# Query and key projections of a gated attention kernel: three rounded products over the whole array in place of float32 products in two column tiles

## The reference

```
xn = layernorm(x)
Q, K, V = xn @ Wq, xn @ Wk, xn @ Wv          # 16 heads of 64, per batch of 1024 tokens
A = softmax(Q K^T / 8) V                      # per batch and head
s = xn + gelu(A) @ Wpost
g = silu(quantise(xn) @ quantise(W).T + bias) # blocks of 32, values on a 6-bit grid
out = x + s * g
```

## Time and profile before

| | |
|---|---|
| median of 3 runs | 1372.78 us (1372.38 to 1373.0) |
| profiled execution, its own time | 1374.83 us |
| its span, first to last instruction | 1372.9 us |
| busy: PE, PEld, DVE, ACT, POOL | 1354.9, 740.5, 1099.5, 768.4, 1169.5 us |
| mean granted PE clock | 0.995 of full speed |
| DMA | 87.61 MB, 64 GB/s |

### The profile page before, as it was taken

The page is one execution under the profiler, slowest core; times in us unless marked ns, Lnnn a source line. Parts: engine busy times, 40 slices in busy tenths (PEclk is TensorE's granted clock), DMA queues, the critical chain, the costliest instruction groups (busy, mean ns, idle before and its releaser), DMA issues.

```text
span 1372.9 us, 26059 instructions
## 1 busy us (share of the span) xinstructions
PE 1354.9 (99%) x9828; PEld 740.5 (54%) x9828; DVE 1099.5 (80%) x1499; ACT 768.4 (56%) x1059; POOL 1169.5 (85%) x548
## 2 busy tenths in 40 slices
PE   7899999999999999999999999999999999999998
PEld 4455555555455555555555555555555555555588
DVE  6688888888888888888888888888888888888533
ACT  3455665554556666455555666555554655555583
POOL 1589999889999989989999999899999999999950
PEclk8999999999999999999999999999999999999999
DMA  2012122111212112121211112121111111222374
GB/s 83 17 42 64 45 62 72 49 57 57 64 42 65 57 45 77 57 64 42 65 56 51 56 57 64 42 64 56 48 58 57 49 27 49 64 77 60 90 258 144
DMA packets 110488, 87.61 MB, mean 64 GB/s; under 512 B 70430, under 2 KB 84510, under 8 KB 110364
## 3 DMA queue, kind: packets, MB, share of 16 engines
q1 hardware_dynamic: 110364, 85.96, 20.7%
HBM read 69.66 MB, written 16.25 MB: 63 GB/s over the span
## 4 chain that ended last, share of the span: by engine, by line
PE 96%; DVE 2%; DMA 1%; issue 0%; ACT 0%; SPq 0%; POOL 0%; DVEq 0%
PE acc L526 32%; PE scores L507 26%; PE peaks L486 13%; PE extra L408 9%; PE scores L516 6%; PE extra L421 4%; PE scores L596 4%; DVE half_maxes L957 1%; PE extra L450 1%; DMA sums<-sum_scratch 1%; PE extra L457 1%; PE extra L432 0%; DMA sum_scratch<-group_sums 0%; DMA x_in<-in_L_attn_X 0%; DVE group_sums L993 0%
## 5 line engine op out<-in xcount | busy, mean ns | idle before, releaser
L840 POOL TENSOR_TENSOR prob_sum<-prob_sum,probs 128x1024 f32<-128x1024 f32 x384 | 915.1, 2383 | 89.3 <-ACT probs L711 49.3
L957 DVE TENSOR_REDUCE half_maxes<-peaks 128x2 f32<-128x1024 f32 x504 | 616.2, 1223 | 182.0 <-PE peaks L486 176.3
L711 ACT ACTIVATE probs<-scores 128x1024 f32<-128x1024 f32 x357 | 355.7, 1024 | 474.5 <-PE scores L516 464.8
L526 PE MATMUL acc<-probs,vals 128*64 128x512 f32 x2048 | 486.1, 595 | 0.0
L526 PEld LDWEIGHTS acc<-probs,vals 128*64 128x64 f32 x2048 | 139.0, 137 | 234.8 <-issue 225.9
L486 PE MATMUL peaks<-k_hi,q_hi 64*128 64x512 f32 x1008 | 233.3, 457 | 4.5 <-DVE half_maxes L957 4.1
L486 PEld LDWEIGHTS peaks<-k_hi,q_hi 64*128 64x128 f32 x1008 | 95.5, 184 | 208.6 <-issue 142.6
L507 PE MATMUL scores<-q_hi,k_hi 64*128 64x512 f32 x1024 | 203.4, 393 | 0.0
L507 PE MATMUL scores<-q_hi,k_lo 64*128 64x512 f32 x1024 | 203.3, 392 | 0.0
L507 PE MATMUL scores<-q_lo,k_hi 64*128 64x512 f32 x1024 | 202.7, 391 | 0.0
L840 POOL TENSOR_TENSOR prob_sum<-probs 128x1024 f32<-128x1024 f32 x64 | 153.5, 2399 | 57.0 <-ACT probs L711 57.0
(11 more groups left out here) (156 smaller groups left out, 923.0 us busy)
## 6 DMA issues: line engine op xcount, KB each, us to landing
max_rep<-max_scratch SPq DMA_DIRECT2D x62, 512.0 KB, 4.0
inv_sum<-inv_scratch SPq DMA_DIRECT2D x128, 128.0 KB, 2.9
att_scratch<-att SPq DMA_DIRECT2D x48, 256.0 KB, 2.3
probs<-att_scratch SPq DMA_DIRECT2D x8, 512.0 KB, 5.0
max_scratch<-turned SPq DMA_DIRECT2D x252, 1.0 KB
sums<-sum_scratch SPq DMA_DIRECT2D x128, 8.0 KB, 2.1
xTs<-att_scratch SPq DMA_DIRECT2D x4, 512.0 KB, 3.6
out_dram<-xn SPq DMA_DIRECT2D x8, 256.0 KB, 3.3
```

Source lines behind the costliest of these rows:

```text
L526: last = mm(acc[own[h], :], vals[(s // 2) % 2][:, j, own[h]], probs[j][:, h, :], start=(k == 0), stop=(k == KT - 1), tile_position=col[h])
L711: sa.activation(probs[j][:, :, :], src[:, :, :], ACT.Exp, scale=DH ** -0.5).then_inc(probs_ready, 1)
L840: gp.tensor_tensor(prob_sum[s % 2][:, :, :], before[:, :, :], probs[order(s)[j]][:, :, :], ALU.add).then_inc(probs_summed, 1)
L957: v.tensor_reduce(half_maxes[:, :, f // 2, f % 2], peaks[:, :, :], AX.X, ALU.max).then_inc(peaks_read, 1)
```

## The change

Four things are changed together.

- **Projections.** For every pair but the first, the queries and keys are projected as three float32r products over the whole array (hi·hi, weights hi·x lo, weights lo·x hi) that accumulate in the bank, three instructions in all, in place of float32 products in two column tiles, four instructions. Values stay as they are.
- **Splits.** x and the two weights are split into a rounded part and a remainder. At the start ACT rounds all of x of batch 0 and both weights, and POOL subtracts three tiles of 128 x 1024. At each of the three turns to a new batch, ACT rounds two halves and DVE subtracts two halves.
- **Memory and order at the turn of a batch.** There is one transposed x in place of four, so the next batch's transposes move from pairs 4 and 5 to pair 6 of the batch (rounds 1 and 3 of its half-1 step), and the first query projection of the new batch moves behind `weigh`. `w_q` and `w_k` share memory with the last two attention blocks, the squares go to `xn`, and of the first eight loads of attention blocks, which stood one a step and then two and one, one stays at step 56, three go to step 61 and four to step 62.
- **First step.** The twelve peaks of step 0 are made three a round, not four, four, two, two. The joining of the maxima of step 1 moves from round 1 to round 2.

```diff
-            if r == 1 and n % HP in (4, 5) and n // HP + 1 < B:
-                before.append(("x", n // HP + 1, n % HP - 4))
+            turned_now = n % HP == HP - 2 and n // HP + 1 < B
+            if r in (1, 3) and turned_now:
+                before.append(("x", n // HP + 1, r // 2))
...
-                before.append(("q", n + 2, 0))
+                (behind if turned_now else before).append(("q", n + 2, 0))
...
     def fills(s, r):
-        if s == 0 and r < 2:
-            return [(1, 4 * r + i) for i in range(4)]
+        if s == 0:
+            return [(1 + k // 8, k % 8) for k in range(3 * r, 3 * r + 3)]
...
-                for p in {NS - 3: (5, 6), NS - 2: (7,)}.get(s, (s - NS + 8,)):
+                for p in {NS - 8: (0,), NS - 3: (1, 2, 3), NS - 2: (4, 5, 6, 7)}.get(s, ()):
...
+                if n == 0:
+                    weights = w_q if name == "q" else w_k
+                    pe.wait_ge(w0_loaded, 48)
+                    has_xT(0, half)
+                    for h in (0, 1):
+                        last = mm(w[own[h], :], weights[:, h * DH:(h + 1) * DH], xT[:, halves[half]],
+                                  start=True, stop=True, tile_position=col[h])
+                else:
+                    if n // HP == 0:
+                        pe.wait_ge(first_split, 3)
+                    else:
+                        pe.wait_ge(x_split, 2 * (n // HP) - 1 + half)
+                    w_hi, w_lo = (wq_hi, wq_lo) if name == "q" else (wk_hi, wk_lo)
+                    for i, (left, right) in enumerate(((w_hi, xT_hi), (w_hi, xT_lo), (w_lo, xT_hi))):
+                        last = mm(w[:, :], left[:, at:at + P], right[:, halves[half]], start=(i == 0), stop=(i == 2))
...
+            def round_xT(use):
+                _, b, half = use
+                is_read(act, use)
+                sa.copy(xT_hi[:, halves[half]], xT[:, halves[half]]).then_inc(x_rounded, 1)
...
+            act.wait_ge(xT_ready, 2)
+            sa.copy(xT_hi[:, :], xT[:, :]).then_inc(x_rounded, 2)
+            act.wait_ge(w0_loaded, 48)
+            act.wait_ge(w_loaded, 48)
+            for dst, weights in ((wq_hi, w_q), (wk_hi, w_k)):
+                sa.copy(dst[:, :], weights[:, :]).then_inc(w_rounded, 1)
...
-                    if half == 1 and r == 1 and n % HP in (4, 5) and later < B:
-                        copy_xT_later(("x", later, n % HP - 4))
+                    if half == 1 and r in (1, 3) and n % HP == HP - 2 and later < B:
+                        copy_xT_later(("x", later, r // 2))
+                    if half == 1 and r == 2 and n % HP == HP - 2 and later < B:
+                        round_xT(("x", later, 0))
+                    if half == 0 and r == 0 and n % HP == HP - 1 and later < B:
+                        round_xT(("x", later, 1))
...
+            pool.wait_ge(x_rounded, 2)
+            gp.tensor_tensor(xT_lo[:, :], xT[:, :], xT_hi[:, :], ALU.subtract).then_inc(first_split, 1)
+            for k, (hi, lo, weights) in enumerate(((wq_hi, wq_lo, w_q), (wk_hi, wk_lo, w_k))):
+                pool.wait_ge(w_rounded, k + 1)
+                gp.tensor_tensor(lo[:, :], weights[:, :], hi[:, :], ALU.subtract).then_inc(first_split, 1)
...
+            def low_x(use):
+                _, b, half = use
+                dve.wait_ge(x_rounded, 2 * b + half + 1)
+                v.tensor_tensor(xT_lo[:, halves[half]], xT[:, halves[half]], xT_hi[:, halves[half]], ALU.subtract).then_inc(x_split, 1)
...
+                    if half == 0 and r == 0 and n % HP == HP - 1 and later < B:
+                        low_x(("x", later, 1))
...
+                    if half == 1 and r == 2 and turned_now:
+                        low_x(("x", later, 0))
+                    if half == 1 and r == 3 and turned_now:
+                        low(("q", n + 2, 0))
```

More of the change, by code:

```diff
@@ L105, in gated_attention_kernel @@
         sem = lambda n: ctx.enter_context(nc.semaphore(n))
-        w_q, w_k, w_v = (sb(f"w_{n}", [P, HD]) for n in "qkv")
-        xT = [sb(f"xTs{b}", [P, S]) for b in range(B)]
+        w_v = sb("w_v", [P, HD])
+        xT = sb("xTs", [P, S])
         with ExitStack() as rounded:
@@ L116, in gated_attention_kernel @@
         rows_back = [sb(f"rows_back{z}", [P, HALF]) for z in (0, 1)]
+        split_back = [sb(f"split_back{k}", [P, S]) for k in range(6)]
         maxima, turned = sb("maxima", [P, SQ], F32R), sb("turned", [P, SQ])
@@ L157, in gated_attention_kernel @@
         flat = lambda a: a[:, :, :].rearrange("p a b -> p (a b)")
-        back = [flat(x_in), flat(squares), xT[0][:, :], xT[1][:, :], xT[2][:, :], xT[3][:, :], w_q[:, :], w_k[:, :],
+        back = [flat(x_in), xT[:, :]] + [split_back[k][:, :] for k in range(6)]
+        back += [
                 q_hi_back[0][:, :], q_lo_back[0][:, :], k_hi_back[0][:, :], k_lo_back[0][:, :],
@@ L420, in project_v @@
                         tokens = half * HALF + t * P + h * DH
-                        last = mm(w[own[h], t * P:(t + 1) * P], xT[n // HP][:, tokens:tokens + DH], w_v[:, at:at + P],
+                        last = mm(w[own[h], t * P:(t + 1) * P], xT[:, tokens:tokens + DH], w_v[:, at:at + P],
                                   start=True, stop=True, tile_position=col[h])
@@ L632, in square @@
                 act.wait_ge(centred, p + 1)
-                sa.activation(squares[:, t0:t0 + nt, :], x_in[:, t0:t0 + nt, :], ACT.Square).then_inc(squared, 1)
+                sa.activation(xn[b][:, t0:t0 + nt, :], x_in[:, t0:t0 + nt, :], ACT.Square).then_inc(squared, 1)
             def root(p):
@@ L671, in copy_xT @@
                 is_filled(act, use)
-                sa.copy(xT[b][:, halves[half]], bank(use)).then_inc(xT_ready, 1)
+                sa.copy(xT[:, halves[half]], bank(use)).then_inc(xT_ready, 1)
             def copy_xT_later(use):
@@ L676, in copy_xT_later @@
                 is_filled(act, use)
-                sa.copy(xT[b][:, halves[half]], bank(use)).then_inc(extra_read, 1)
+                sa.copy(xT[:, halves[half]], bank(use)).then_inc(extra_read, 1)
+            def round_xT(use):
+                _, b, half = use
+                is_read(act, use)
+                sa.copy(xT_hi[:, halves[half]], xT[:, halves[half]]).then_inc(x_rounded, 1)
             def high(use):
@@ L745, in _ @@
                         copy_v(("v", n + 1, 0))
-                    if n + 2 < NP and half == 1 and r == 3 and not gates_now:
+                    if n + 2 < NP and half == 1 and r == 3 and not gates_now and not (n % HP == HP - 2 and later < B):
                         high(("q", n + 2, 0))
@@ L759, in _ @@
                         copy_acc(s - 1)
+                    if half == 1 and r == 3 and n % HP == HP - 2 and later < B:
+                        high(("q", n + 2, 0))
                     if half == 1 and r == 1:
@@ L1050, in _ @@
                         low(("q", 1, 0))
-                    if r == 1 and s > 0 and s + 1 < NS:
+                    if r == (1 if s > 0 else 2) and s + 1 < NS:
                         join_maxima(s + 1)
@@ L1058, in _ @@
                         low((("k", n + 1, 0), ("k", n + 1, 1), ("q", n + 1, 1))[r])
-                    if n + 2 < NP and half == 1 and r == 3:
+                    turned_now = n % HP == HP - 2 and later < B
+                    if n + 2 < NP and half == 1 and r == 3 and not turned_now:
                         low(("q", n + 2, 0))
-                    if r == 1 and s > 0 and s + 1 < NS:
+                    if r == (1 if s > 0 else 2) and s + 1 < NS:
                         turn_squares(s + 1)
```

22 lines of the change are left out of this document (11 added, 11 removed).

## The result

The changed kernel takes 1380.3 us (median of 5 runs, 1379.4 to 1382.8), the kernel before 1373.0 beside it (5 runs): ratio 1.005, 95% interval 1.0038 to 1.0062. It is slower by 7.3 us, where 3.1 were forecast. The median lies 0.3 above the forecast's range of 1350 to 1380; the ratio put on the 1372.8 of the prediction gives 1379.6, just inside it. Its profiled execution is the longest of the five, 1382.8 us with a span of 1381.0, against 1372.9 before: +8.1.

The account below looks back on a forecast made before the run. The prediction took PE, busy 99% of the span, to bound the kernel. Shape changes +4.8, first step -2.5, turns +0.6 and tail +0.2 make +3.1 us on 1372.8: 1375.9 us, range 1350 to 1380.

Parts of the forecast that it names:

- The price of a change of shape: On PE around each projection: entering and leaving the whole array costs time, 0.04 us lost a projection, +4.8 us in all.
- From peak to `weigh` 1.23 becomes 1.22: Sign in PE's timeline: the time from the peak's start to that of `weigh` goes from 1.23 to 1.22 us.
- The two rivals in which a border is free: Projections on PE: only column tiles or float32 have borders, 1351.7 us, chance 0.20; only row tiles, 1357.8 us, chance 0.08.
- The plain count: Rival for projections on PE: matmul lengths alone count, 0.21 us less a projection, 1345.7 us, chance 0.03.
- The first step: Step 0: three peaks a round cut PE's idle time, two waits of some 1.3 us left; -2.5 us, between -4 and 0.
- The covers named for the splits: At the start: ACT's roundings (3.2 to 3.5 us) and POOL's subtractions (7.1 us) fit within their existing waits.
- The turns: Three batch turns: added ACT roundings and DVE subtractions cost +0.2 us each, +0.6 in all, between 0 and +3.
- No wait over 0.5 us on x's split: Sign at the turns to a new batch: no wait for the split of x exceeds 0.5 us.
- The tail: End of kernel: up to three more 512 KB loads ahead of the post weights cost +0.2 us, between 0 and +2.
- The rival of a new wait: Subtractions, single transposed x or bunched loads stall PE 1 or 2 us at each turn and the tail: 1379 to 1384, chance 0.09.
- The sum: Whole kernel: +4.8 - 2.5 + 0.6 + 0.2 = +3.1 us, giving 1375.9 us; chance 0.60.

Follow-up runs that it names:

- experiment 4: Changed kernel with one float32 product in column tiles, on the rounded parts only, in place of the three whole-array products: 1377.4 us, ratio 1.0024 to the kernel before.
- experiment 1: Changed kernel with its late loads of attention blocks spread (one, three, three, one over steps 56, 60, 61, 62): 1377.4 us, ratio 1.0022 to the kernel before.
- experiment 6: Changed kernel with loads spread and one float32 product in column tiles on the rounded parts, remainder products left out: 1375.7 us, ratio 1.0006 to the kernel before.
- experiment 5: Kernel before with its 124 projections as one float32 product over the whole array in place of two in column tiles: 1394.6 us, ratio 1.0145.
- experiment 8: Changed kernel with loads spread and 93 projections cut in two by `weigh`, one product ahead and two behind: 1481.2 us, ratio 1.0775 to the kernel before.
- experiment 3: Kernel before with only step 0's peaks made three a round and step 1's maxima joined in round 2: 1371.7 us, ratio 0.9981.
- experiment 2: Kernel before with only the changed kernel's bunched schedule of loads (three in step 61, four in step 62): 1377.8 us, ratio 1.0023.
- Experiment 10: Changed kernel with loads spread and DVE's subtraction for the new batch's first queries one reduction later: 1376.4 us, ratio 1.0024 to the kernel before.
- experiment 9: Experiment 8 with ACT's rounding and DVE's subtraction of even steps' projections moved to the next round's start: 1511.9 us, ratio 1.1014 to the kernel before.

## Why the prediction came out as it did

**The price of a change of shape: right.** The forecast was "0.34 + 0.23 + 0.33 + 0.05 = 0.95 against 0.91". The medians over the steady part are 0.328 for the peak, 0.896 for the three products and 1.868 for `weigh`, against 0.329, 0.909 and 1.817 before: +0.036 each, 4.4 us for 121, where +4.8 was said. Not all of it reaches the time: at the last step the changed kernel is 2.5 us behind experiment 4 and experiment 1 is 2.9 behind experiment 6 (counted from step 1), because peaks and scores take 1.5 to 2 us less. The prediction let what PE loses go straight into the time. That PE waits less for DVE when its other work is longer would explain this; it is not shown. "From peak to `weigh` 1.23 becomes 1.22" held. The two rivals in which a border is free are out: the peak took 0.32 and `weigh` 1.87, and experiment 5 shows the border with the type held toward `weigh`, experiment 8 prices a second entrance and exit at 0.20. The plain count is out for the same reason. By the rule of the Trainium skill (TensorEngine Tiling (Array Packing), Tiling Modes and Key Properties: 128x128 is a configuration of its own, and changing the mode drains the engine) the runs agree, with 0.10 us to leave, 0.11 to enter with 128 columns of weights and 0.05 with 64.

**The first step: the size right, by luck in part.** "I take -2.5 us, between -4 and 0": -1.8 at the first `weigh` of step 1 and -2.2 at its first peak in the changed kernel, -2.6 by the time of experiment 3. The two waits that were said to be left are there, at 1.32 and 1.41 us. But the sum "5.1 - 2 x 1.3" took all of PE's idle time for waits that the new order ends. Idle time fell by 1.0 us (5.1 to 4.1); three waits became two, and the smaller ones stayed. The rest came from the clock, which the forecast had only as a way to reach 4. Of the twelve kept traces the nine with three peaks a round have no second stretch of half clock in step 0; of the three with four a round two have it, and experiment 5, with no such stretch, begins step 1 at 58.08 like the changed kernel. So the order seems to make the stretch rarer, and the old order can do without it too. The covers named for the splits held: step 1 begins at 58.1, 0.6 later than the "near 57.5" of the text, and no projection of the first steps waits for a split. That experiment 3 gains another 1.5 us after step 1 was not forecast, and it may be no gain: the traces of the kernel before and of experiment 2, whose code is the same up to the loads, drift by up to 1 us between the same steps. Differences between single traces are no better than that.

**The turns: too small.** The forecast was +0.6 in all, between 0 and +3. Experiment 6 set against experiment 3 step by step gives some 0.8, 1.3 and 0.8 us for the three turns, 2.9 in all, at the top of the bound; with the 0.9 that lies outside them it is 3.8 in the traces, 3.4 by the times. At the turn the query projection stands behind `weigh`, so ACT rounds it late. DVE, in its fixed order, waits for that while a reduction that could start stands behind it, and a peak waits for the reduction. The timeline of DVE at the first turn:

```profile
318.93 0.69 DVE L991 TENSOR_TENSOR q_lo<-extra,q_hi 128x512 fp32r<-128x512 f32 x1 [1.87 <-ACT q_hi L705]
319.54 1.22 DVE L1003 TENSOR_REDUCE half_maxes<-peaks 128x2 f32<-128x1024 f32 x1
```

The timeline of PE there:

```profile
320.81 0.49 PE L503 MATMUL peaks<-k_hi,q_hi 64*128 64x512 f32 x2 [0.47 <-DVE half_maxes L1003]
```

The prediction counted DVE's 0.68 of work and not the 1.87 for which it stands idle ahead of it. "No wait over 0.5 us on x's split" held: there was none on the split. Experiment 10 takes this wait away and wins back a third of a microsecond a turn, so the rest of the turns' cost stays open. The query projection ahead of `weigh` was not tried.

**The tail: the step that failed.** The forecast counted "+0.2, between 0 and +2", from the post weights' own arrival. They did arrive in time: the closing stretch starts right behind the last `weigh`, as said. But the bunched loads cost 3.8 us by the ratios of the changed kernel and experiment 1, 3.2 by experiment 2, and 5.4 in the profiled executions. What was missed is not in the loads' own length. Ahead of the post weights the same queue has the store of step 61's inverse (the prediction called it the last one, but two more follow). SP waits for its landing before it issues the spread; behind four loads of 512 KB this small store takes 6.6 us instead of 2.1, and with it every issue behind it is late, down to the sums' store and the last operands of the closing stretch. The sum counted three transfers against the slack of one consumer, where it should have followed SP's order to its end. How much of the hold reaches the time depends on more than its length: holds of 6.6, 6.7 and 6.2 us made the closing stretch 5.1, 6.5 and 2.2 us longer (the changed kernel, experiments 2 and 4), and what decides it was not tested. The rival of a new wait named the bunched loads, at 1379 to 1384; it wanted them together with waits of 1 or 2 us at each turn, and the measured 1380.3 lies in its span, with the tail as the larger part.

**The sum.** In the spans the changed kernel is 3.0 us behind when the closing stretch begins, against 2.9 forecast without the tail, and the stretch adds 5.1: 8.1, or 7.3 in the medians. The 3.0 are not made up as forecast. Experiment 3 stands at -3.3 at the last step; experiment 6, which adds the splits and the turns, is 3.8 behind it; and the changed kernel is another 2.6 behind experiment 6, for its projections. So the turns and splits cost 3.2 more than the 0.6 counted, the projections 2.2 less than the 4.8, and the first step gave 0.8 more than the 2.5. That these errors cancel is luck; the excess of 4.2 us over the forecast is about the tail's.

## What to carry to other kernels

Count a change of array shape as work: here a float32 product in the tiles of its neighbours at 0.91 us beats three float32r products over the whole array at 0.90, because the neighbour pays 0.05 more; in the whole kernel that is 2 to 3 us. When loads are moved on a queue, follow the queue's order past them to every store whose landing the issuing engine waits for, and not only to the consumer of the last load. An edit made of several parts can hide a good one: the first step's order, with the clock that went with it, is worth 2.6 us by itself, and was the only part here that made the kernel faster.

## What the runs showed of the hardware that had not been expected

- The inverse's small store behind four 512 KB loads on SP's queue let its follower go after 6.6, 6.7 and 6.2 us (the changed kernel, experiments 2 and 4), behind one load after 1.8 (experiment 1). In the changed kernel it landed 0.2 us after the last of the four loads.
- One float32 product of 128 columns over the whole array, with 512 columns streamed, takes 1.05 us with its entrance and exit, its neighbour being float32 too (experiment 5).
- Splitting 93 projections cost 18.5 us in changes of shape and 85 in waits: the late end of a group is worth far more than the borders it adds, where two other engines work on it in a fixed order (experiments 8 and 9).
- The stretch at half clock after step 0's waits is not fixed by the code: with four peaks a round two traces have it (the kernel before, experiment 2) and one with three such waits has not (experiment 5). With three a round none of nine has it, although two waits of 1.32 and 1.41 us are left.
